# First quantised feed-forward part moved into the loop of the first attention, with two score banks in place of four

## The reference, cut to what matters

```python
x = x + attn_a(layernorm(x))      # 16 heads of 8, latent keys, causal softmax
x = x + ffn(layernorm(x))         # the part "p" that is moved
x = x + attn_b(layernorm(x))      # "forget" attention, a scan over the 8 batches
x = x + ffn(layernorm(x))         # the same weights again: part "q"
x = x + conv(layernorm(x))        # "conv"

def fp4_quant_dequant(x):         # blocks of 16 channels
    scale = maximum(max(abs(xb)) / 6.0, 1e-12)
    return GRID[searchsorted(MID, abs(xb / scale))] * sign(xb) * scale

def ffn(x):                       # 128 -> 352 -> 128
    gate = fp4(x) @ fp4(w_gate).T
    h = silu(gate) * (fp4(x) @ fp4(w_up).T)
    return fp4(h) @ fp4(w_down).T
```

## Time and profile before

| | |
|---|---|
| median of 3 runs | 2007.7 us (2006.86 to 2008.63) |
| the profiled execution, its own time | 2009.31 us |
| its span in the profile | 2007.5 us |
| busy: PE, DVE, ACT, POOL | 1718.6, 1388.4, 961.2, 452.2 us |
| granted TensorE clock, mean | 0.934 |

### The profile page before, as it was taken

How to read it: one execution, slowest core, us unless ns; L and a number is a source line. 1 busy time by engine, 2 the same in 40 slices (tenths; PEclk the granted TensorE clock), 3 DMA queues, 4 the chain that set the end, 5 groups by cost and what they waited for, 6 DMA issues and landing times.

```text
span 2007.5 us, 33581 instructions
## 1 busy us (share of the span) xinstructions
PE 1718.6 (86%) x10818; PEld 1398.8 (70%) x10875; DVE 1388.4 (69%) x3623; ACT 961.2 (48%) x2583; POOL 452.2 (23%) x344
## 2 busy tenths in 40 slices
PE   6999986676556899999989899999968999999997
PEld 5888884434344677777777777777746777777776
DVE  4655579869995767767777655556466687686684
ACT  3444432223222575665665553434406656656654
POOL 2200010100002334334334100000013343343440
PEclk9999987756777999999999999999989999999999
DMA  4000000000010000000000000000000000000000
GB/s 143 0 0 0 0 1 0 0 0 1 0 53 0 3 3 1 3 3 2 3 2 2 4 1 0 0 0 0 0 1 2 3 1 3 4 3 3 3 1 24
DMA packets 15107, 13.79 MB, mean 7 GB/s; under 512 B 11286, under 2 KB 14138, under 8 KB 14650
## 3 DMA queue, kind: packets, MB, share of 16 engines
q1 hardware_dynamic: 15034, 12.88, 2.0%
HBM read 9.74 MB, written 1.05 MB: 5 GB/s over the span
## 4 chain that ended last, share of the span: by engine, by line
PE 43%; DVE 33%; issue 17%; ACT 4%; POOL 1%; DVEq 1%; POOLq 0%; ACTq 0%
PE bank L1630 5%; PE bank L1761 4%; DVE arena_ffn L954 3%; DVE arena_attn L969 3%; PE bank L1662 3%; DVE ssq L962 3%; PE bank L1799 3%; PE bank L1748 3%; PE bank L1650 3%; DVE arena_ffn L950 3%; DVE probT L718 3%; PE bank L1803 2%; DVE nmaxF L711 2%; PE bank L1819 2%; PE bank L1641 2%
## 5 line engine op out<-in xcount | busy, mean ns | idle before, releaser
L555 POOL TENSOR_TENSOR arena_ffn<-arena_ffn 128x1024 f32<-128x1024 f32 x60 | 141.3, 2355 | 502.2 <-DVE arena_ffn L954 502.2
L718 DVE COPY probT<-bank 128x512 f32<-128x512 f32 x288 | 196.4, 682 | 25.7 <-PE bank L1641 25.5
L551 POOL TENSOR_TENSOR inv<-ssq,mhalf 128x16 f32<-128x16 f32 x64 | 186.3, 2911 | 75.7 <-DVE ssq L963 75.3
L1650 PE MATMUL bank<-vF,probT 128*128 128x64 f32 x1536 | 195.8, 270 | 4.9 <-DVE probT L718 2.6
L539 POOL TENSOR_TENSOR rstd<-var,mhalf 128x2 f32<-128x2 f32 x32 | 22.3, 698 | 778.2 <-DVE var L673 778.2
L1650 PEld LDWEIGHTS bank<-vF,probT 128*128 128x128 f32 x1536 | 186.5, 192 | 11.8 <-DVE probT L718 11.5
L1630 PE MATMUL bank<-arena_setup 128*128 128x192 f32 (+1 forms) x1024 | 171.6, 300 | 6.8 <-ACT arena_setup L1406 5.2
L711 DVE TENSOR_REDUCE nmaxF<-bank 128x2 f32<-128x384 f32 (+1 forms) x192 | 114.5, 596 | 88.2 <-PE bank L1630 88.2
L1630 PEld LDWEIGHTS bank<-arena_setup 128*128 128x128 f32 x1024 | 154.3, 191 | 12.3 <-issue 1.0
L1458 ACT ACTIVATE arena_conv<-bank,nmaxF 128x192 f32<-128x192 f32 x256 | 105.6, 420 | 114.6 <-DVE nmaxF L711 111.2
L1340 ACT ACTIVATE prob<-bank,nmax 128x128 f32<-128x128 f32 (+1 forms) x256 | 88.9, 429 | 124.8 <-DVE nmax L711 124.8
(11 more groups left out here) (281 smaller groups left out, 4114.7 us busy)
## 6 DMA issues: line engine op xcount, KB each, us to landing
packF<-in_packF SPq DMA_DIRECT2D x1, 3122.0 KB
arena_history<-in_packG SPq DMA_DIRECT2D x1, 2560.0 KB, 8.8
HS<-XH SPq DMA_DIRECT2D x32, 63.5 KB
X<-in_x_tiled SPq DMA_DIRECT2D x1, 1024.0 KB, 5.0
out_dram<-X SPq DMA_DIRECT2D x8, 128.0 KB, 1.9
arena_setup<-in_const_masks_a SPq DMA_DIRECT2D x1, 512.0 KB, 5.5
arena_setup<-in_const_masks_f SPq DMA_DIRECT2D x1, 512.0 KB
HS<-XH SPq DMA_DIRECT2D x32, 0.2 KB
```

The source lines that it names most:

```text
L551: pool.tensor_tensor(inv[:, t, :, 0], ssq[:, t, :, 0], mhalf[:, 0:16], ALU.pow).then_inc(sems["inv_ready"], 1)
L555: pool.tensor_tensor(t1[:, t], t1[:, t], t2[:, t], ALU.add).then_inc(sems["rope_sum"], 1)
L718: dve.tensor_copy(probT[:, u % 2], bank[4 + u % 2][:]).then_inc(sems["pt_copied"], 1)
L1650: ins = pe.matmul(o, probT[:, u % 2, n * P:(n + 1) * P], val, start=first, stop=(kt == keys // P - 1), skip_group_check=True)
```

## The change

The stage `ffn4` is gone. Its work is now a part `p` with semaphores of its own, run like `q`. In attention batch i, DVE quantises h of `p` batch i-2 and x of `p` batch i-1, one link of each chain per step, between the maxima and copies. PE does the up products of i-2 in step 0, the transposes in step 10, the down product in step 11 and the gate products of i-1 in step 13. ACT applies silu at the end of the batch, with a table load to silu and one back to exp. Six of the eight batches finish `p` inside the loop; batch 6 and most of 7 finish in steps 0 and 1 of the forget stage, banks 5 to 7. To free banks 2 and 3 for `p`, the scores take banks 0 and 1 in turn. The weights are quantised in attention batch 0 and transposed in batch 1, the decay tables are made by ACT ahead of batch 6, and the taps by POOL during it.

The core of the diff. DVE, the attention batch and the forget step:

```diff
-            def attn_a(v, i, norm, weights):
+            def attn_a(v, i, norm, weights, end, x, h):
...
-                        attn_max(v, i, s, len(heads), keys, nmax, 4)
+                        attn_max(v, i, s, len(heads), keys, nmax, 2)
                     if s >= 2:
                         attn_copy(v, i, s - 2)
-                    if norm and s == 2:
+                    if h is not None and s == 1:
+                        q_h(vp, h, P_BANKS)
+                        qh = Quantiser(vp, h_job(vp, h))
+                    if h is not None and s in (2, 3):
+                        qh.step(qch)
+                    if x is not None and s < Q_LINKS:
+                        qx.step(qch)
+                    if h is not None and 2 <= s < Q_LINKS:
+                        qh.step(qch)
+                    if s == Q_LINKS:
+                        if h is not None:
+                            qh.finish(qch).then_inc(vp.sem("hq_ready"), 1)
+                        if x is not None:
+                            qx.finish(qch).then_inc(vp.sem("xq_ready"), 1)
+                    if norm and s == Q_LINKS + 1:
                         first_stats(i + 2)
-                    if norm and s == 5:
+                    if h is not None and s == A_UNITS:
+                        q_end(vp, h, bank[2][:, 0:T])
+                    if norm and s == A_UNITS + 1:
                         first_apply(i + 2)
-                    if weights and s < Q_LINKS + 1:
-                        quantise_weights(s)
+                    if weights and 2 <= s < Q_LINKS + 3:
+                        quantise_weights(s - 2)
+                    if end and s == 2:
+                        setup_gates()
+                    if end and s == 4:
+                        setup_rest()
...
-                normalise(v, i, ch)
+                norm_stats(v, i, ch)
+                if h is not None:
+                    norm_apply(vp, h)
+                norm_apply(v, i)
...
                 for k in range(NB + 4):
                         if k < NB:
                             forget_step(vf, k)
-                        q_quantise(vq, vf, inside(k - 2), inside(k - 1))
+                        hs = [(vp, NB - 2 + k)] if k < 2 else [(vq, k - 2)] if inside(k - 2) is not None else []
+                        xs = [(vp, NB - 1, vals[n - 2])] if k == 0 else [(vq, k - 1, vf)] if inside(k - 1) is not None else []
+                        q_quantise(vq, hs, xs)
```

ACT, the end of an attention batch:

```diff
                 if more:
                     take_keys(v, n)
-                    for g in range(4):
+                    for g in range(2):
                         take_queries(v, n, g)
                     take_attn_values(v, n)
+                if x is not None:
+                    prime(ACT.Silu)
+                    q_silu(vp, x, P_BANKS)
+                    prime(ACT.Exp, 1)
```

PE, what stands between the units of a batch (`between`), and the loop:

```diff
+                    if h is not None and s == 0:
+                        q_up(vp, h, P_BANKS)
+                    if end and s == 1:
+                        setup_gates()
+                    if end and s == 3:
+                        setup_rest()
+                    if h is not None and s == 10:
+                        q_transpose(vp, h, P_BANKS)
+                    if x is not None and s == 10:
+                        q_tokens(vp, x, bank[6])
+                    if h is not None and s == 11:
+                        q_down(vp, h, bank[2])
...
+                        pe.wait_ge(sems["exp_ready"], v.at("exp_ready", i, A_UNITS - 1))
+                        project_queries(0)
+                    if x is not None and s == A_UNITS + 1:
+                        if end:
+                            pe.wait_ge(setup_dve, N_DVE_ALL)
+                        q_gate(vp, x, 0, P_BANKS)
+                        if h is not None:
+                            pe.wait_ge(vp.sem("down_used"), vp.at("down_used", h, 1))
+                        q_gate(vp, x, 1, P_BANKS)
...
-                attention(v, i, A_UNITS, 4, 4, maskb, scores, values, between)
+                attention(v, i, A_UNITS, 4, 2, maskb, scores, values, between)
...
-                    with pe.Fori(0, NB - 1) as i:
-                        attn_a(v, i, True)
-                    attn_a(v, NB - 1, False)
+                    attn_a(v, 0, True, False, None, None)
+                    attn_a(v, 1, True, True, 0, None)
+                    with pe.Fori(2, NB - 1) as i:
+                        attn_a(v, i, True, False, i - 1, i - 2)
+                    attn_a(v, NB - 1, False, False, NB - 2, NB - 3)
```

More of the change, by code:

```diff
@@ L589, in _ @@
                 if kind == "attn_a":
+                    vp = vals[n + 1]
                     stage_copy(0)
@@ L781, in quantise_weights, with __init__, step, finish @@
                 ins.then_inc(setup_dve, 1)
+            class Quantiser:
+                def __init__(self, v, job):
+                    self.dsts, self.src, self.first, self.nb, self.free = job
+                    self.k, self.last = 0, 0
+                def step(self, ch):
+                    if self.last:
+                        ch.wait(self.last)
+                    self.last = ch.mark(quantise_step(self.k, self.src, self.first, self.nb))
+                    self.k += 1
+                def finish(self, ch):
+                    assert self.k == Q_LINKS
+                    ch.wait(self.last)
+                    self.free()
+                    at = self.first
+                    for dst in self.dsts:
+                        m = dst.shape[1]
+                        ins = dve.tensor_tensor(dst, blocks(qv[:, at * FBL:(at + m) * FBL]),
+                                                qscale[:, at:at + m].broadcast_to([P, m, FBL]), ALU.mult)
+                        at += m
+                    return ins
             def quantise(jobs, mark, wait):
@@ L836, in h_job, with q_h, q_quantise @@
                         h[:].rearrange("p t f -> p (t f)"), 0, NT * FI // FBL, free)
[L838 to L850, removed]
[L851 to L861 removed]
+            def q_h(v, i, banks):
                 for t in range(NT):
                     dve.wait_ge(v.sem("up_ready"), v.at("up_ready", i, t + 1))
[L864 to L868 removed]
+                    dve.tensor_tensor(h[:, t], silu[:, t], bank[banks[t]][:, 0:FI], ALU.mult).then_inc(v.sem("h_ready"), 1)
+            def q_quantise(v, hs, xs):
+                jobs = [h_job(vj, i) for vj, i in hs] + [x_job(vj, i, vin) for vj, i, vin in xs]
                 if not jobs:
@@ new lines, in q_up, with q_out @@
+            def q_up(v, i, banks):
+                for t in range(NT):
+                    pe.wait_ge(v.sem("silu_ready"), v.at("silu_ready", i, t + 1))
+                    pe.matmul(bank[banks[t]][:, 0:FI], xqT[:, t * P:(t + 1) * P], wguT[:, 1, 0:FI], start=True,
+                              stop=True).then_inc(v.sem("up_ready"), 1)
+            def q_out(v, i, vf, k):
+                q_transpose(v, i, Q_BANKS)
+                if k < NB:
+                    pe.wait_ge(vf.sem("down_used"), vf.at("down_used", k, 1))
+                else:
+                    pe.wait_ge(v.sem("down_used"), v.at("down_used", i, 0))
+                q_down(v, i, bank[7])
@@ L1924, in conv_taps, with q_gates @@
+            def q_gates(v, i):
+                q_tokens(v, i, bank[4])
+                for t in range(NT):
+                    q_gate(v, i, t, Q_BANKS)
+                q_up(v, i, Q_BANKS)
             def conv_taps(v, i, vin):
@@ L1982, in project_queries @@
             def project_queries(g):
-                pe.matmul(bank[g][:, 0:T], qproj[:, g * P:(g + 1) * P], xT[:], start=True, stop=True).then_inc(sems["misc_ready"], 1)
+                for m in range(2):
+                    k = 2 * g + m
+                    ins = pe.matmul(bank[g][:, m * T:(m + 1) * T], qproj[:, k * P:(k + 1) * P], xT[:], start=True, stop=True)
+                ins.then_inc(sems["misc_ready"], 1)
             def project_attn_values(v, i):
@@ L2034, in _ @@
                 v = vals[n]
-                if kind.startswith("mlp") or kind in ("q", "conv") or kind == "win" and not begins(n):
+                if kind.startswith("mlp") or kind in ("p", "q", "conv") or kind == "win" and not begins(n):
                     continue
```

328 lines of the change are left out of this document (138 added, 190 removed).

## The result

The changed kernel takes 1995.4 us (median, 1992.94 to 2002.77); the kernel before, run beside it, 2008.9 (2006.86 to 2011.7). The ratio is 0.9935, 95% interval 0.9921 to 0.9949: faster, but by 13 us where the prediction says 49. The profiled execution took 1996.95 us (span 1995.2), 12.4 less than that of before. So 36.8 us of the predicted gain are missing.

The account below looks back on a forecast made before the run. PE was taken to bound the attention loop, DVE the setup and feed-forward stretch. -105.7 + 41.3 + 15.2 = -49.2 on 2009.3 gives 1960.1, at the median 1958.5 us; range 1943 to 1982.

Parts of the forecast that it names:

- The stage removed: From the end of the last attention batch to forget step 0 on DVE, all time goes away: -105.7 us.
- batches 2 to 5: Attention loop: each batch grows by 1.1 in steps 0 to 2 and 3.9 in steps 10 to 13, +5.0 us.
- the 1.1 of the two banks: Attention steps 0 to 2: scores of unit 2 wait for earlier exponentials with two banks, +1.1 us a batch.
- The other batches: Attention batches 0, 1, 6 and 7, priced at +1.5, +6.5, +8.3 and +5.0 us.
- Batch 1: Attention: two banks, x transposes and gates, setup matmuls, weight transposes and a wait for the gate weights' copy, +6.5 us.
- batch 6: Attention: +5.0 as in the loop, and +3.3 for decay tables ACT makes ahead of its first exponentials; +8.3 us.
- The forget head: Start of the forget stage: 1.5 ahead of step 0, 7.6 in step 0, 6.1 in step 1; +15.2 us together.
- The prediction's own last sentence: Wrong above all if waits in steps 10 to 13 were long: PE needs hq, ACT's copies, then DVE's residual.
- (b): PE's idle time takes more new work, or the forget clock starts full: 1944 us; chance 0.17.
- (a): DVE becomes the pace of the attention's middle units, 3.2 us more a batch: 1978 us; chance 0.18.
- (d): Two score banks chain PE, DVE and ACT, each unit pays; slower, 2035 us at 0.8 per unit; chance 0.04.
- (c): ACT is late for each attention batch's first exponentials through table switches, +18 us: 1977 us; chance 0.05.

Follow-up runs that it names:

- e4: Kernel before with only the attention scores in two PSUM banks in place of four, query projections two to a bank; 2019.5 us, ratio 1.0048.
- e11: Changed kernel with silu replaced by a plain copy and the table primers left out in the attention; 1994.4 us, ratio 0.9929.
- e6: Changed kernel with five extra score products on PE in the lull of every lin batch; 1977.6 us, ratio 0.9846.
- e1: Changed kernel with the forget-stage down product waiting for each transposed half of hq in turn; 1965.7 us, ratio 0.9777.
- e14: Changed kernel with the wait for hq split only in the last four down products of the forget stage; 1975.6 us, ratio 0.9841.
- e13: Changed kernel with five extra score products in the lull of the last lin batch alone; 1987.8 us, ratio 0.9902.
- e2: Changed kernel with thirty chained fills (35.1 us) on DVE at the very start; 2033.7 us, ratio 1.0112.
- e3: Changed kernel with thirty chained fills (35.1 us) on DVE before the forget stage; 2032.7 us, ratio 1.0110.
- e7: Changed kernel with one fill (1.2 us) on DVE just ahead of lin's first mask; 1993.9 us, ratio 0.9943.
- e8: Changed kernel with the forget-stage wait split and two fills (2.3 us) on DVE ahead of lin's first mask; 1966.9 us, ratio 0.9795.
- e12: Changed kernel with the forget-stage wait split and two fills (2.3 us) on DVE ahead of lin's first batch's last feature map; 1962.3 us, ratio 0.9781.
- e9: Changed kernel with the forget-stage wait split and five extra score products in each lin batch's lull but the last; 1981.3 us, ratio 0.9874.
- e5: Kernel before with only the single wait for both hq halves in the forget-stage down product; 2034.2 us, ratio 1.0130.
- e10: Kernel before with five extra score products in the lull of each lin batch but the last; 2021.6 us, ratio 1.0070.

## Why the prediction was wrong, by its own steps

**The stage removed, -105.7, and batches 2 to 5, +5.0 each:** right. Measured +4.8; e4 shows the 1.1 of the two banks by itself, e11 that the table loads cost nothing there. The drain that the Trainium skill gives ("ScalarE: Activation LUTs", "What ACT_TABLE_LOAD costs") does not show: in the rows of e11's section the exponentials begin 1.29 us after their load does.

**The other batches, sizes off by 3.8 in all,** of which batches 2 to 5 give back 0.7: the attention grew by 44.4 in place of 41.3. Batch 1 grew by 9.6 (6.5 predicted), batch 6 by 9.6 (8.3), batch 7 by 4.6 (5.0), batch 0 by 1.3 (1.5). The prediction has no dip of the clock in the attention. In e6 batch 6 ran at clock 1.00 and took 41.3 us, 8.0 more than before; the dip of the changed kernel (0.96) adds 1.6. Its term was right. Batch 1 took 41.5 us at clock 0.96 in e6 and 43.2 at 0.92 in the changed kernel. No run shows it at 1.00, so how much of its 3.1 is clock stays open.

**The forget head, +15.2, off by 3.3.** Measured 1.5 ahead of step 0, as predicted, then +9.3 for step 0 (7.6) and +7.7 for step 1 (6.1). With the wait split these two are +7.0 and +6.3. The sizes were right for the old waits; what was missing is the single wait, 0.65 in each, and the lower clock that came with it (0.62 and 0.64, in e1 0.64 and 0.70). In e1 the clock was low ahead of step 0, another 3.5 us.

**The step that failed is one that the prediction does not have.** It says that step 0 "gets what step 2 has" and prices it with rows of the old down product. `q_down` was not the old code: it has one wait, for both halves. The prediction's own last sentence named the waits of PE for hq and for ACT's copies, but only for attention steps 10 to 13, where PE shows none over 0.1 us in batches 2 to 5. In the forget stage it costs 7.9 us by the first window stage, though e1 came 3.0 us later to step 0, so 10.9 in all: some 6.5 for ten waits of 0.65, the rest goes with the lower clock.

**And it took the lead at forget step 2 for the lead at the end.** Behind the first window stage e1 keeps its 43 us to the end (42.8); the changed kernel loses another 22.7: 3.2 in the window stages, 17.0 in lin, 2.0 in the second window stages, 0.5 at the end. The sum of the prediction ends at forget step 2; for all that stands behind it has no term, and it says nothing of the clock there. This is the largest part of the miss. Nothing there was edited. Its lulls are the same; that they are followed by a lower clock comes from the last forget steps (e14) and through the lulls (e6, e13). Of the 36.8 us missing, e1 returns 30.5: 42.9 against 49.2 predicted. The 6.3 left are 2.6 in the attention, 3.5 of clock ahead of forget step 0, and 0.2 in all the rest.

**The rivals.** None came true. (b) hoped for a better clock in the forget stage; it rose from 0.50 and 0.51 to 0.62 and 0.64 in the first two steps, but with more work in them, and none of the time came back. In (a) and (d) the middle units would have slowed; they keep 2.33 us. (c) fell with e11.

**Open:** what carries the state from the last forget steps to lin, and why one lull is followed by the fall and the next, of the same length, is not. Long delays do not reset it (e2, e3), the short ones of e7, e8 and e12, which were to test a short cycle, did not reach PE, filling the lulls before changes what the last one does (e9), and a few executions of one program differ (e5, e7, e10).

## What to carry to other kernels

Read a moved or merged helper against the code it replaces wait by wait: a wait for n things ahead of a loop in place of one inside costs the last producer's time in every call, and it may be needed in only one of the places that share the helper. A gain that reaches a stage kept at the clock's edge by short lulls is not safe; look at the granted clock of each stage behind, fill such lulls or shorten them, but all of them (with the last one left out, the medians of e9 and e10 are 16 and 14 us above those of the same kernels without fills), and test a suspected wait alone before blaming the clock for the whole. When a delay is meant as a probe, make sure first that the engine it should hold up has no slack.

## What the hardware showed that I had not expected

A lull of 1.43 us in a stream that keeps PE busy is enough for the clock to fall from 2.4 to 1.2 GHz, and equally not enough, in the same instructions of two kernels. Once down, PE stayed at 1.2 GHz for 34.1 us of lin's last batch, from 1429.6 to 1463.7, though it was busy for 34.6 of the 36 us from 1428 to 1464; in the three slow batches before it, behind lulls of 1.79 us, it was back after 6.8. The Trainium skill ("TensorE: Matmul & The Clock Gate", section "HAM oscillation — how this bites in real kernels") tells of waits that recur in every step of a loop, throttle the clock each time, and are cured by a loop order that keeps the engine at work. Its waits are longer ones, for DMA. e6 agrees with the cure, at lulls of 1.43 and 1.79 us: five useless products in each took 17 us off lin. That a busy engine stays at the low clock for so long, the section does not say.
